# Rotary columns as an even and an odd pack, each read twice, in place of four packs

## The reference

```
q_lat = (x @ Wq_down).reshape(b, t, H, L)        # H = 16 heads, L = 64
q_c = einsum('bthl,ld->bhtd', q_lat, Wq_up_c)    # 8 columns of each head
q_e = einsum('bthl,ld->bhtd', q_lat, Wq_up_e)    # 8 rotary columns of each head
x1 = x[..., 0::2];  x2 = x[..., 1::2]
rot = stack((-x2, x1), axis=-1).reshape(x.shape)
q = concatenate([q_c, q_e * cos + rot(q_e) * sin], axis=-1)
```

## Time and profile before

| | |
|---|---|
| median of 3 runs | 1241.82 us (1235.46 to 1245.02) |
| profiled execution | 1240.2 us, span 1238.5 us |
| TensorE, VectorE, ScalarE, GpSimd busy | 81%, 61%, 54%, 41% of the span |
| first pack of the loop starts | 363.96 us |
| last value tile's ScalarE copy | 464.05 us |

### The profile page before, as it was taken

One profiled execution on the slowest core, in us unless ns is written; L12 is line 12 of the kernel. 1 busy time (PEld: TensorE's weight loads), 2 busy tenths in 40 slices (PEclk: granted clock), 3 DMA queues, 4 the chain that ended last, 5 costly groups with the idle time before them and its releaser, 6 DMA issues. The chain is left out here.

```text
span 1238.5 us, 24304 instructions
## 1 busy us (share of the span) xinstructions
PE 999.4 (81%) x8630; PEld 721.2 (58%) x8630; DVE 757.0 (61%) x1547; ACT 666.5 (54%) x1587; POOL 501.6 (41%) x684
## 2 busy tenths in 40 slices
PE   5227888888699997999999999999883889888840
PEld 1126676776598884555555555555462667667740
DVE  3994333333267847888888888988078333333338
ACT  2733333343257642888888787888576334333320
POOL 1625566565355540223232232332200556565630
PEclk9658999999859995999999999999795899999985
DMA  8713544444337673346455464452186222222249
GB/s 307 238 67 115 197 151 168 150 163 166 108 131 231 212 219 89 87 107 134 108 123 117 105 131 100 109 115 64 44 277 238 75 81 82 82 79 84 80 134 317
DMA packets 100659, 172.89 MB, mean 140 GB/s; under 512 B 15872, under 2 KB 64512, under 8 KB 100544
## 3 DMA queue, kind: packets, MB, share of 16 engines
q1 hardware_dynamic: 86912, 134.09, 37.2%
q0 software_dynamic: 13632, 37.24, 9.0%
HBM read 101.55 MB, written 69.47 MB: 138 GB/s over the span
## 5 line engine op out<-in xcount | busy, mean ns | idle before, releaser
L1886 ACT ACTIVATE spare<-h_psS 128x512 f32<-128x512 f32 x576 | 306.5, 600 | 86.0 <-PE h_psS L1793 84.4
L1911 DVE TENSOR_REDUCE h_part<-h_psM 128x2 f32<-128x1024 f32 (+3 forms) x256 | 249.0, 1015 | 12.5 <-PE h_psM L1772 12.1
L1941 POOL TENSOR_SCALAR_AFFINE_SELECT spare<-spare 128x256 f32<-128x256 f32 x256 | 99.9, 409 | 294.9 <-ACT spare L1886 294.9
L887 POOL DMA_INDIRECT ys<-m_y,m_slot_u x142 | 140.5, 989 | 153.3 <-ACT m_y L974 123.1
L909 PE MATMUL m_psG<-wgu,m_x_hi 128*128 x568 | 196.5, 428 | 1.2 <-DVE m_x_lo L983 1.2
L909 PE MATMUL m_psY<-wdn,m_h_hi 128*128 x568 | 129.0, 309 | 67.2 <-DVE m_h_lo L999 58.6
L1820 PE MATMUL h_psO<-spare,a_VP 128*17 128x256 f32 (+3 forms) x3072 | 166.2, 335 | 7.4 <-ACT spare L1874 7.2
L993 DVE TENSOR_TENSOR m_h<-m_act_g,m_psG 128x256 f32<-128x256 f32 x142 | 59.4, 418 | 169.5 <-ACT m_act_g L967 147.0
L881 POOL DMA_INDIRECT m_xg<-xn,m_slot_u x138 | 134.0, 971 | 47.2 <-issue 37.2
L1793 PE MATMUL h_psS<-h_QT,h_KT 49*128 49x512 f32 x720 | 150.8, 404 | 2.5 <-ACT spare L1886 2.3
L967 ACT ACTIVATE m_act_g<-m_psG 128x256 f32<-128x256 f32 x142 | 55.5, 391 | 173.7 <-PE m_psG L909 121.6
(11 more groups left out here) (232 smaller groups left out, 1567.7 us busy)
## 6 DMA issues: line engine op xcount, KB each, us to landing
xn<-spare SPq DMA_DIRECT2D x16, 512.0 KB, 7.1
wg_d<-wgu SPq DMA_DIRECT2D x16, 512.0 KB
results<-ys SPq DMA_DIRECT2D x16, 512.0 KB, 5.3
a_KD<-spare SPq DMA_DIRECT2D x32, 256.0 KB, 3.0
a_OD<-spare SPq DMA_DIRECT2D x128, 64.0 KB, 2.5
wgu<-wg_d SPq DMA_DIRECT2D x16, 512.0 KB, 10.5
last<-ys SPq DMA_DIRECT2D x16, 512.0 KB, 7.2
h_KT<-a_KD SPq DMA_DIRECT2D x60, 132.0 KB
```

The lines of the kernel that those rows point to most:

```text
L887: pool.indirect_dma_start(ys_d[:, :], bass.IndirectOffsetOnAxis(ap=slot_u[:, b, 1:2], axis=0), y[b % R][:, :], None).then_inc(stored[b % R ...
L1886: act.activation(prob[k % NP][:, h, :], psS[x % NS][:, :], ACT.Exp).then_inc(s_read, 1)
L1911: m = dve.tensor_reduce(out, psM[k % NM][:, :, at:at + n], AX.X, ALU.max, negate=True)
L1941: m = pool.affine_select(block, block, [[0, 2], [1, P]], ALU.is_ge, 0.0, 0, -1)
```

## The change

The four rotary packs (`ke`, `ks`, `qe`, `qs`) become two: `even` holds the even rotary columns of keys (rows 0 to 63) and queries (rows 64 to 127), `odd` the odd ones. VectorE reads each twice, each time against another table: even x cos and even x sin, odd x -sin and odd x cos. GpSimd's sums then give the rotated even and the rotated odd columns. The swapped weights and their casts go. A folded result is written in three pieces for keys and queries (plain, even, odd) where it was one on ScalarE and two on VectorE. The tables are four of 128x1024; two are loaded where the old two were, the other two by four transfers in "project". A store of `even` or `odd` is four transfers of 64 partitions, to `a_KD` and `a_QD`, where `ke` had two of 128. Each pack has its own PSUM bank. The order of the work within a group changes on TensorE, ScalarE, VectorE and SyncE.

```
-PACKS = ("ke", "ks", "kc", "qe", "qs", "qc")
-BASE = {"kc": 0, "ke": 1, "qc": 2, "qe": 3, "ks": 4, "qs": 5}
+PACKS = ("even", "odd", "kc", "qc")
+BASE = {"kc": 0, "qc": 1, "even": 2, "odd": 3}
+STORES = {"even": 64, "odd": 64, "kc": 32, "qc": 32}
...
+        odd = [sb(f"rope{i}", [P, HALF]) for i in range(3)] + [area.place("p_rope3", [HALF], area.WGU1 + used + 2 * HALF)]
...
+            of, base = 1 - w, BASE[("qc", "kc")[w]] * P
+            parts = src.rearrange("p (g k d) -> p k g d", g=H, k=2)
+            pieces = [(parts[:, 0], [k[:, c, base:base + P].rearrange("p (g d) -> p g d", g=H) for k in w_eff])]
+            for o, name in enumerate(TURNED):
+                at = BASE[name] * P + of * P // 2
+                pieces.append((parts[:, 1].rearrange("p g (i o) -> p o g i", o=2)[:, o],
+                               [k[:, c, at:at + P // 2].rearrange("p (g i) -> p g i", g=H) for k in w_eff]))
+            return made.scale if w == 0 else 1.0, pieces
...  (SyncE)
+                        if k in TURNED:
+                            row, n = part * DH + DH // 2 + DH // 4 * TURNED.index(k), DH // 4
+                            for i, D in enumerate((KD, QD)):
+                                sp.dma_start(D[b * H:(b + 1) * H, row:row + n, at:at + HALF],
+                                             tile[k][j][64 * i:64 * i + 64, :].bitcast(F32)).then_inc(stored[k][j], 16)
...
+                for i in range(4):
+                    sp.dma_start(odd[i][:, :], early.rope_d[2 + i // 2, :, i % 2 * HALF:i % 2 * HALF + HALF]).then_inc(odd_in, 16)
...
-                    sp.wait_ge(p_read, NP * g + 3)
+                    sp.wait_ge(c_read, 2 * g + 1)
                     store("kc", g)
                     sp.wait_ge(elo_done, 2 * g + 1)
-                    store("ke", g)
-                    sp.wait_ge(p_read, NP * g + 6)
+                    store("even", g)
+                    sp.wait_ge(c_read, 2 * g + 2)
                     store("qc", g)
                     if g + 5 < NG:
                         fetch(g + 5)
                     sp.wait_ge(elo_done, 2 * g + 2)
-                    store("qe", g)
+                    store("odd", g)
...  (TensorE)
+                    if g >= 1:
+                        if k in TURNED:
+                            pe.wait_ge(multiplied, 4 * (g - 1) + 2 * n + 2)
+                        else:
+                            pe.wait_ge(c_read, 2 * (g - 1) + n - 1)
+                    three(pe, psP[n][:, :], w[0], w[1], x).then_inc(packed, 1)
...
                 for g in range(NG):
                     pe.wait_ge(xlo_done, 2 * g + 2)
-                    for n in range(3):
+                    for n in range(2):
                         pack(g, n)
                     if g + 1 < NG:
                         turn(g + 1)
-                    for n in range(3, NP):
+                    for n in range(2, NP):
                         pack(g, n)
...
+                        value(g, n - 2)
+                    value(g, 2)
                     value(g, 3)
...  (ScalarE)
                 for g in range(NG):
-                    high_c("kc", g)
                     if g + 1 < NG:
                         high(g + 1)
-                    high_e("ke", g)
+                    high_e("even", g)
+                    high_c("kc", g)
+                    value_out(g, 0)
+                    high_e("odd", g)
+                    high_c("qc", g)
+                    value_out(g, 1)
                     if g + 2 < NG:
                         normal(g + 2)
-                    value_out(g, 0)
-                    value_out(g, 1)
-                    high_c("qc", g)
+                    value_out(g, 2)
+                    value_out(g, 3)
                     if g + 4 < NG:
                         first(g + 4)
-                    high_e("qe", g)
-                    value_out(g, 2)
-                    value_out(g, 3)
                     if g + 3 < NG:
                         deviate(g + 3)
...  (VectorE)
+                def turn_e(g):
                     at = (g % 2) * HALF
+                    tables = [early.rope[:, i, at:at + HALF] for i in range(2)] + [odd[2 * i + g % 2][:, :] for i in range(2)]
+                    for i, tiles in enumerate((t1, t2)):
+                        dve.wait_ge(packed, NP * g + i + 1)
+                        for n, k in enumerate(TURNED):
+                            if g >= 1 and i == 0:
+                                dve.wait_ge(summed, 2 * (g - 1) + n + 1)
+                            dve.tensor_tensor(tiles[k][:, :], psP[i][:, :], tables[2 * i + n], ALU.mult).then_inc(multiplied, 1)
...
                 for g in range(NG):
                     if g + 2 < NG:
                         invert(g + 2)
-                    turn_e("ke", g)
-                    low_c("kc", g)
+                    turn_e(g)
                     if g + 1 < NG:
                         low(g + 1)
-                    turn_e("qe", g)
+                    low_c("kc", g)
                     low_c("qc", g)
                     if g + 3 < NG:
                         combine(g + 3)
...  (GpSimd)
-                pool.wait_ge(flo_done, 8)
-                for k, s in (("ke", "ks"), ("qe", "qs")):
...
-                                pool.tensor_copy(out[:, :, way], src[:, :, 1 - way]).then_inc(w_ready, 1)
                 add(2)
                 add(3)
                 for g in range(NG):
-                    rotate("ke", g)
-                    rotate("qe", g)
+                    rotate("even", g)
+                    rotate("odd", g)
                     if g + 4 < NG:
                         add(g + 4)
```

More of the change, by code:

```diff
@@ L1194, in project @@
         two = lambda n, s, d=F32: [sb(f"{n}{j}", s, d) for j in range(2)]
-        ALL = ("ke", "qe", "kc", "qc")
+        ALL, TURNED = tuple(STORES), ("even", "odd")
         rope, wc, wct, up, down = early.rope, early.wc, early.wct, early.up, early.down
-        w_eff = [sb(f"w_eff{k}", [P, CC, 4 * C + E], F32R) for k in range(2)]
+        w_eff = [sb(f"w_eff{k}", [P, CC, 3 * C + E], F32R) for k in range(2)]
         size = PER * C
@@ L1220, in project @@
         ones, mask_made, g_made, ghi_done, glo_done = (sem(n) for n in ("ones", "mask_made", "g_made", "ghi_done", "glo_done"))
-        folded, fhi_done, flo_done, w_ready = (sem(n) for n in ("folded", "fhi_done", "flo_done", "w_ready"))
+        folded, fhi_done, flo_done = (sem(n) for n in ("folded", "fhi_done", "flo_done"))
         part_done, xs_done, x_done, counted, var_done, std_done, rs_done, xn_done, turned, xhi_done, xlo_done = (
@@ L1233, in fold @@
             if w == 2:
[L1234 to L1237, removed]
+                return 1.0, [(src, [k[:, c, 2 * C:3 * C] for k in w_eff])]
+            of, base = 1 - w, BASE[("qc", "kc")[w]] * P
[6 more added lines that the diff above has]
+            return made.scale if w == 0 else 1.0, pieces
         nc.clear_and_free_semaphores(held)
@@ L1338, in _ @@
                         turn(g + 1)
-                    for n in range(3, NP):
+                    for n in range(2, NP):
                         pack(g, n)
-                        if g == 0 and n == 3:
-                            pe.wait_ge(flo_done, 10)
-                        value(g, n - 3)
+                        if g == 0 and n == 2:
+                            pe.wait_ge(flo_done, 14)
+                        value(g, n - 2)
+                    value(g, 2)
                     value(g, 3)
@@ L1406, in _ @@
                 for n in range(2 * CC):
-                    src, scale, (h, _) = fold(n)
-                    act.wait_ge(folded, n + 1)
-                    act.activation(h, src, ACT.Copy, scale=scale).then_inc(fhi_done, 1)
+                    high_fold(n)
                 first(2)
@@ L1721, in fetch @@
                     sp.dma_start(wgu[0][:, at].bitcast(F32), weights_d[:, at]).then_inc(wg_in, 16)
-                for tiles in stored.values():
+                for k, tiles in stored.items():
                     for landed in tiles:
-                        sp.wait_ge(landed, 32 * (sh.B * T // HALF // 2))
+                        sp.wait_ge(landed, STORES[k] * (sh.B * T // HALF // 2))
                 for p in range(pairs.AHEAD, NK - 1):
@@ L1874, in out @@
                     act.activation(OT[p % 2][:, :, :], psO[:, :, :], ACT.Copy).then_inc(o_read, 1)
-                for tiles in stored.values():
+                for k, tiles in stored.items():
                     for landed in tiles:
-                        act.wait_ge(landed, 32 * (sh.B * T // HALF // 2))
+                        act.wait_ge(landed, STORES[k] * (sh.B * T // HALF // 2))
                 act.wait_ge(row_turned, 1)
@@ L2028, in rope_tables @@
     emb = np.concatenate((freqs, freqs), axis=-1)
-    sign = np.where(np.arange(D) % 2 == 0, np.float32(-1), np.float32(1))
-    tables = np.stack((np.cos(emb), np.sin(emb) * sign)).astype(np.float32)
```

(4 more changed lines are left out.)

89 lines of the change are left out of this document (39 added, 50 removed).

## The result

Twenty runs of each gave a median of 1247.5 us for the changed kernel (1242.9 to 1255.7) and 1236.4 us for the one before (1231.2 to 1245.0): ratio 1.0093, interval 1.0074 to 1.0113, or 11.1 us slower by the medians and 11.5 by the ratio. The median before had come out 5.4 us lower than the three runs the prediction had.

What follows compares the result with a forecast made beforehand. TensorE was taken to bound the projection at 12.53 us a group, then a 15.06 us ring through the other engines; 7.4 + 1.2 + 2.0 + 1.7 = +12.3 gave 1252.5 to 1254.1, stated as 1253.0 us, range 1240 to 1263.

Steps and rivals of the forecast that it cites:

- Bound before, and the 2.80 us freed: Projection loop: TensorE without slack at 12.53 us a group; two packs fewer free 2.80, so it needs 9.35.
- The ring: Projection groups: chain through VectorE, GpSimd, ScalarE and back to invert, held by add, sets 15.06 us a group, 2.53 more.
- Loop: Projection's eight groups, first product to GpSimd's last low part: 102.5 us against 95.15, +7.4.
- the two rings through TensorE: Late projection groups: circle through value tile and the pack of even, 10.5 us each.
- Ahead of the loop: Block's start to VectorE's first product: smaller folded pieces and add(2) meeting combine(1), +1.2 us, bounds -0.8 and +2.8.
- Clock: TensorE in the projection: waits of 3.1 and 2.6 us a group lower its clock; 0 to +5.6, taken +2.0 us.
- The end: Projection's last stores on SyncE: four odd transfers behind qc's two, +1.1 to +2.4, taken +1.7 us.
- The port rival: Projection loop: add doesn't hold invert, groups take 13.0 us, 1244 to 1246 us in all; chance 0.15.
- the unchanged pace of 12.5: Projection loop: an overlooked wait holds the group at 12.5 us, nothing gained or lost, 1243 us; chance 0.02.
- VectorE was never the bound: Rival for the projection loop: VectorE becomes the bound, some 10.3 us a group, 1226 us; chance 0.05.
- The low clock: Rival for the projection loop: TensorE's clock stays low, 17.5 us a group, 1262 to 1270 us; chance 0.10.

Runs made afterwards that it cites:

- Half `add`: Changed kernel with GpSimd's add for groups 4 to 7 over half its rows; ratio to the kernel before 1.0072.
- new order: Changed kernel with invert behind the products, the second pair's load in the next block and ScalarE's order in a group rearranged; ratio to the kernel before 0.9844.
- four matmuls: Changed kernel with each pack of keys and queries in four matmuls in place of six; ratio to the kernel before 1.0124.
- invert late: Changed kernel with VectorE's invert(g+2) moved after turn_e and low; ratio to the kernel before 1.0033.

## Why the prediction came out right, step by step

- **Bound before, and the 2.80 us freed.** Right: with the ring broken the pace is 9.6 beside the 9.35 worked out.
- **The ring.** Right in place and size: 15.06 forecast, 15.01 measured, with the hold at L1462 (L1483 now) of 2.17 or 2.18 us in four groups. Half `add` and the move of `invert` show that both are on it. ScalarE's wait ahead of `high_e("even")`, forecast at 4.7, is 3.20 there and 1.29 ahead of `high`, which waits for the turn.
- **Loop.** +7.4 forecast, +7.69 measured; the two rings through TensorE took 10.69 and 10.88 for 10.5. The measured 7.69 includes what the clock cost, for which the forecast had a term of its own.
- **Ahead of the loop.** +1.2 forecast, +0.70 measured. The 12 pieces took 1.47 us of ScalarE's queue (1.05 before, 2.2 forecast), and `add(2)` did meet `combine(1)`: its four operations took 3.76 us where 1.7 is usual. Without the casts `shift` was free, as said.
- **Clock.** The fall was right, its price wrong. TensorE's two waits of one group, then the stage table, both of the changed kernel (TensorE's busy time and count, clock, DMA share, GB/s):

```profile
417.76 0.51 PE L1068 MATMUL p_psV<-p_w_eff,p_x_hi 128*128 128x264 f32 x2 [1.30 <-ACT a_lx L1420]
...
421.06 0.81 PE L1068 MATMUL p_psV<-p_w_eff,p_x_hi 128*128 128x264 f32 x2 [2.31 <-ACT a_lx L1420]
```

```profile
416.00:420.00 4.00, 1.45 (x10) 0.95 0.20 47
420.00:424.00 4.00, 2.94 (x10) 0.50 0.84 276
424.00:428.00 4.00, 4.00 (x19) 0.69 0.62 212
428.00:432.00 4.00, 4.00 (x24) 1.00 0.00 0
...
452.00:456.00 4.00, 4.00 (x26) 1.00 0.63 208
...
460.00:464.00 4.00, 4.00 (x21) 1.00 0.88 276
```

In each of groups 0 to 4 it fell to 0.50 (1.2 GHz) around waits of up to 1.3 and 2.3 us (3.1 and 2.6 had been forecast, with TensorE counted at full clock), where the slack covered it. In groups 5 and 6, whose ring it would have lengthened, TensorE waited 1.23 us once in each and ran at 1.00: the term of +2.0 was nothing here. It isn't always. In the profile of the unaltered kernel on the other chips the clock came back 0.77 us behind group 5's first product (411.29, 410.52), where above it had come back 0.14 us ahead of it. The third product waited for TensorE, and the distance to the next group was 11.31 for 10.69:

```profile
412.34 0.69 DVE L1503 TENSOR_TENSOR p_t_even<-p_psP,p_rope 128x512 f32<-128x512 f32 x1 [0.53 <-PE p_psP L1068]
```

The Trainium skill, in "TensorE: Matmul & The Clock Gate", tells under its second failure mode of a kernel whose TensorE idled briefly between groups of matmuls, lost and regained its clock, and paid for it in throughput. The loss and the return in each group are to be seen here; the price was nothing in one profile and 0.6 us in the other, as the ring and not TensorE set the pace.
- **The end.** The term that was mis-sized: +1.7 forecast, +4.70 measured. It took SyncE as idle when the last stores came. It had missed that SyncE's queue is late: the eight loads, four for each of two heads, that group 6 puts into it are worth about 2 of the missing 3.0 (the run with the load moved). It had also let a store of 64 rows cost down to half; each took 0.58 to 0.63 and followed the last after 0.64, about as one of 128 rows does. The errors, +3.0 here, -2.0 in the clock's term, -0.5 ahead of the loop and +0.3 in it, nearly cancel: +12.3 forecast, +13.1 in the block. The ring was worked out; that the sum came so near was luck. The absolute 1253.0 also stood on a median of the kernel before that came out 5.4 us lower with more runs.
- **The rivals.** The port rival fell by the 2.17 us rows and the pace of 15.0, and with it the unchanged pace of 12.5. VectorE was never the bound: even in the new order it is busy 9.47 where TensorE is busy 9.60 of 9.60. The low clock fell by the pace of 15.0 in place of 17.5, and by the run with four matmuls.

What stays open: why the program takes 1236 us on some chips and 1167 on others while this block keeps its length. Between the two profiles of the changed kernel, 30 us of it lie ahead of the block and 42 behind the attention, so in the two mixtures of experts; I didn't follow it.

## What to carry to other kernels

A kernel can become slower by less work on its fullest engine, if the new order closes a longer circle through the others. Before taking work from the engine that sets the pace, add up the longest circle through the others in their written order, with every short operation that waits at the head of a queue. The gain is the distance to that circle, not to the next engine's busy time. If the circle is longer, reorder first: put what waits for others late, what frees others early.

## What the runs showed of the hardware

- A 128x8 operation on VectorE of 0.14 us was held 2.17 us by a GpSimd sum of 2.38 us over SBUF (changed kernel) and 1.08 by one of 1.29 (half add); it ended each time within 0.03 us of it. Products that read PSUM ran beside the same sum at 0.68 to 0.69 us (invert late).
- A store of 64 rows of 2 KB took SyncE 0.58 to 0.63 us to issue (changed kernel); two of 128 rows took 1.16 to 1.25 (both kernels).
